# A four-layer graph-attention stack: the grid of v from weight lengths in three layers, and another order of sums, fillers and w rows

## What is computed

```
Wh = h @ W
e = u[:, None] + v[None, :]            # u = Wh @ a_src, v = Wh @ a_dst
e = where(e > 0, e, 0.2 * e)
attention = softmax(where(adj > 0, e, -9e15), axis=1)
out = elu(attention @ Wh)
```

## Time and profile before

| | |
|---|---|
| median of 3 runs | 678.42 us (673.24 to 678.65) |
| profiled execution, its own time | 678.56 us |
| span, first to last instruction | 676.5 us, 7526 instructions |
| mean granted TensorE clock | 0.934 |
| busy: TensorE, VectorE, ScalarE, GpSimd | 586.6, 366.5, 278.6, 29.1 us |

### The profile page before, as it was taken

How to read it: one execution, slowest core, us unless ns; L and a number is a source line. 1 busy time by engine, 2 the same in 40 slices (tenths; PEclk the granted TensorE clock), 3 DMA queues, 4 the chain that set the end, 5 groups by cost and what they waited for, 6 DMA issues and landing times.

```text
span 676.5 us, 7526 instructions
## 1 busy us (share of the span) xinstructions
PE 586.6 (87%) x3167; PEld 196.9 (29%) x3167; DVE 366.5 (54%) x515; ACT 278.6 (41%) x297; POOL 29.1 (4%) x27
## 2 busy tenths in 40 slices
PE   5434999998999998999979899988679898999997
PEld 3301222343222333122234122235223231333332
DVE  2876756537656537665644675624599968100001
ACT  1564545433545432544532554432577765200000
POOL 0400000200000100000000000012000000000000
PEclk9556999999999999899997899999699998899999
DMA  9990000000000000000000000000000000000000
GB/s 361 357 360 7 1 0 1 1 0 1 1 1 0 1 1 1 0 1 1 0 1 1 0 1 1 0 1 1 0 0 1 1 0 1 1 0 1 1 0 32
DMA packets 3041, 19.33 MB, mean 29 GB/s; under 512 B 320, under 2 KB 320, under 8 KB 960
## 3 DMA queue, kind: packets, MB, share of 16 engines
q1 hardware_dynamic: 2864, 17.83, 6.7%
q10 hardware_dynamic: 144, 1.03, 0.5%
HBM read 18.33 MB, written 0.52 MB: 28 GB/s over the span
## 4 chain that ended last, share of the span: by engine, by line
PE 64%; DVE 19%; ACT 7%; issue 5%; DMA 2%; POOL 1%; POOLq 0%; DVEq 0%; ACTq 0%
PE PROD L632 14%; PE X L842 8%; PE S L644 8%; PE X L624 8%; PE PROD L842 7%; DVE X L1064 5%; DVE aB L1273 5%; ACT big L362 3%; PE X L523 2%; PE M L610 2%; PE S L857 2%; DMA big<-in_adjT 2%; DVE big L1051 1%; DVE nadj L1172 1%; POOL rr L301 1%
## 5 line engine op out<-in xcount | busy, mean ns | idle before, releaser
L362 ACT ACTIVATE big<-X,v 128x1024 f32<-128x1024 f32 x128 | 137.3, 1111 | 154.9 <-PE X L624 154.4
L1064 DVE SCALAR_TENSOR_TENSOR X<-wB,v,aB 128x1024 f32<-128x1024 f32 x128 | 161.5, 1290 | 71.2 <-ACT big L362 69.8
L632 PE MATMUL PROD<-big,Wh 128*64 128x512 f32 x512 | 130.8, 631 | 3.6 <-ACT big L362 3.4
L624 PE MATMUL X<-nadj,bigI 128*128 128x512 bf16 x256 | 73.4, 391 | 23.9 <-DVE X L1064 23.7
L644 PE MATMUL S<-big,onesf 128*32 128x512 f32 x512 | 68.2, 605 | 5.3 <-ACT big L362 5.3
L632 PEld LDWEIGHTS PROD<-big,Wh 128*64 128x64 f32 x512 | 31.2, 139 | 84.9 <-ACT big L362 45.7
L624 PEld LDWEIGHTS X<-nadj,bigI 128*128 128x128 bf16 x256 | 16.3, 97 | 102.4 <-DVE X L1064 66.3
L842 PE MATMUL PROD<-nadj,Wh 128*64 128x512 f32 x128 | 31.0, 614 | 2.9 <-ACT nadj L458 2.9
L301 POOL TENSOR_TENSOR rr<-var,mhalf 128x8 f32<-128x8 f32 x8 | 16.9, 2114 | 377.2 <-DVE var L965 377.2
L610 PE MATMUL M<-big,level 128*32 128x512 fp8e4 x256 | 19.5, 440 | 15.4 <-ACT big L401 8.6
L842 PE MATMUL PROD<-big,Wh 128*64 128x512 f32 x128 | 31.3, 606 | 0.7 <-ACT big L458 0.6
(11 more groups left out here) (254 smaller groups left out, 583.4 us busy)
## 6 DMA issues: line engine op xcount, KB each, us to landing
big<-in_adjT SPq DMA_DIRECT2D x13, 1024.0 KB, 7.9
aB<-in_adjT SPq DMA_DIRECT2D x3, 1024.0 KB, 9.1
cst<-in_cst ACTq DMA_DIRECT2D x1, 1008.5 KB, 5.6
x<-in_xT SPq DMA_DIRECT2D x1, 512.0 KB, 6.2
out<-x SPq DMA_DIRECT2D x2, 256.0 KB, 2.0
```

The costliest lines, as they stand in the source:

```text
L362: act.activation(prob[:, t % U, :], X[t % 2][:], ACT.Exp, bias=v2[l % 2][:, k:k + 1]).then_inc(p_ready, 1)
L624: last = pe.matmul(X[t % 2][:, hh * BANK:(hh + 1) * BANK], bigI[:], nadj[:, k, half_cols(c, hh)], start=False, stop=True, skip_group_check ...
L632: last = pe.matmul(PROD[c][feat(hh), :], Wh[l % 2][:, k, :], prob[:, t % U, hh * BANK:(hh + 1) * BANK], start=k == 0, stop=k == NB - 1)
L1064: dve.scalar_tensor_tensor(X[t % 2][:], wB[:, cols(c)], v8[l % 2][:, k:k + 1], aB[:, cols(c)], ALU.max, ALU.add).then_inc(x_written, 1)
```

## The change

For the first three attention layers (`l < FIX`) the range of `v` is not found any more. `h` has a bounded length after normalisation, so `|v|` is at most that length times the length of the vector that makes `v` out of `h`. The kernel takes the squares of these weight vectors once, in the load (`weight_squares`), adds them up with one product on TensorE, takes the inverse root on GpSimd, and makes a bound, a step and its inverse for the three layers (`weight_norms`, `value_bounds`, which also give `nvs` and `nvb` for `shift_rows`). `value_levels` then makes `gridz` from `v` in one instruction. The grid is centred, so the constant `win` is shifted by half the span, and `LEAN` moves the result back. The last layer (`l == 3`) keeps the range, in a `value_range` of its own.

In the load `convert(5)` and `convert(6)`, which stood between the steps of the range, move behind layer 0's levels. On TensorE the sums of chunk 0's last pair move behind its products and behind the first two masks of chunk 1 (chunk 1's last pair keeps its order); the fillers ahead of the loop go from 12 to 19; between two loops the numbers of fillers change, and ahead of layer 3 `features` comes before `w_rows`. The hunks left out (...) declare tiles and semaphores.

```diff
@@ -24,6 +24,9 @@
 TOP = LOW + EXPS * 128
 SPAN = WIN * EXPS * 128 * (1 - 2.0 ** -12)
 SLOPE = 0.2
+FIX = 3
+REACH = 8.1
+LEAN = 5.5 * 128
 PARTS = 3
 KR = PARTS * PARTS * EMB
 KPAD = 96
...
@@ -312,6 +327,8 @@
 
             for c in range(NCH):
                 inverse_root(part_of(rr, c), part_of(var, c))
+            pool.wait_ge(normsq_ready, 1)
+            pool.tensor_tensor(norm[:], normsq[:], mhalf[:, 0:FIX], ALU.pow).then_inc(norm_ready, 1)
             for c in range(NCH):
                 below_one(c)
             for lf in (1, 2):
@@ -346,11 +363,11 @@
                     act.activation(wB[:, half_cols(c, hh)], row_bank(n, hh)[:], ACT.Copy).then_inc(wB_ready, 1)
 
             def shift_rows(l):
-                act.wait_ge(nv_param, l + 1)
+                act.wait_ge(nv_param, 1 + l // FIX)
                 for q in range(4):
                     act.wait_ge(nv_psum, 4 * l + q + 1)
                     act.activation(aB[:, q * BANK:(q + 1) * BANK], X[q // 2][:, (q % 2) * BANK:(q % 2 + 1) * BANK],
-                                   ACT.Identity, bias=nv[:, 1:2], scale=nv[:, 0:1]).then_inc(nv_ready, 1)
+                                   ACT.Identity, bias=nvb[:, l:l + 1], scale=nvs[:, l:l + 1]).then_inc(nv_ready, 1)
 
             def exponential(l, c, k):
                 t = NB * (NCH * l + c) + k
@@ -587,13 +604,12 @@
                     last = pe.matmul(EB[c][feat(hh), bb * P:(bb + 1) * P], col, ident, start=True, stop=True)
                 last.then_inc(rb_psum, 1)
 
-            def value_range(l):
-
-                pe.wait_ge(vext_ready, l + 1)
+            def value_range():
+
+                pe.wait_ge(vext_ready, 1)
                 pe.transpose(X[1][0:2, 0:P], vext[:], ident).then_inc(vrow_psum, 1)
-                if l:
-                    repeat(X[0], 3)
-                pe.wait_ge(diag_ready, l + 1)
+                repeat(X[0], 3)
+                pe.wait_ge(diag_ready, 1)
                 pe.matmul(X[1][:, 0:2], onef2[:], diag2[:], start=True, stop=True).then_inc(range_psum, 1)
 
             def top_levels(l):
@@ -708,6 +724,9 @@
                 centre(n)
             for n in range(NCH):
                 variances(n)
+            pe.wait_ge(wsq_ready, 1)
+            pe.matmul(X[1][:, 0:FIX], onesf[0:F, 0:1].broadcast_to([F, P]), wsq[:], start=True,
+                      stop=True).then_inc(norm_psum, 1)
             for n in range(NCH):
                 features(n)
             for n in range(NCH):
@@ -715,9 +734,7 @@
                 w_broadcast(n)
 
             for l in range(GAT):
-                if l == 0:
-                    value_range(0)
-                else:
+                if l == 3:
                     repeat(X[0], 9)
                 top_levels(l)
                 if l:
@@ -725,7 +742,7 @@
                 if l == 2:
                     root_broadcast(0)
                 if l:
-                    repeat(M, 12)
+                    repeat(M, 19)
                 pe.wait_ge(nv_ready, 4 * (l + 1))
                 mask(l, 0, 0)
                 mask(l, 0, 1)
@@ -734,7 +751,7 @@
                         k = 2 * p
                         if p == 0 and l == 2:
                             pe.wait_ge(h0_ready, c + 1)
-                        if p == NB // 2 - 1:
+                        if c and p == NB // 2 - 1:
                             pe.wait_ge(p_ready, NB * (NCH * l + c + 1))
                             sums(l, c, k + 1)
                         products(l, c, k)
@@ -742,10 +759,11 @@
                         if p < NB // 2 - 1:
                             mask(l, c, k + 2)
                             mask(l, c, k + 3)
-                            sums(l, c, k + 1)
                         elif c == 0:
                             mask(l, 1, 0)
                             mask(l, 1, 1)
+                        if c == 0 or p < NB // 2 - 1:
+                            sums(l, c, k + 1)
                         if c == 0:
                             if p == 0 and l:
                                 w_broadcast(2 * l + 1)
@@ -781,19 +799,21 @@
                 reciprocal_rows(l, 1)
                 if l < 2:
                     centre_old(2 * l + 3)
-                repeat(X[0], 2)
-                if l < 2:
+                    repeat(X[0], 3)
                     centre(2 * l + 3)
-                if l < 3:
                     w_rows(2 * l + 2)
-                if l < 2:
                     variances(2 * l + 3)
                     repeat(X[0], 2)
+                    features(2 * l + 3)
+                if l == 2:
+                    repeat(X[0], 12)
+                    features(2 * l + 3)
+                    w_rows(2 * l + 2)
                 if l < 3:
-                    features(2 * l + 3)
                     w_broadcast(2 * l + 2)
-                    repeat(X[0], 2)
-                    value_range(l + 1)
+                    repeat(X[0], 3 if l == 2 else 7)
+                if l == 2:
+                    value_range()
             first_turn(0)
             mlp(1)
             repeat(X[1], 3)
@@ -1013,30 +1033,65 @@
 
                 par = l % 2
                 v = uv[par][:, :, 1]
+                if l < FIX:
+                    signal(dve.scalar_tensor_tensor(gridz[:], v.unsqueeze(2).broadcast_to([P, NB, WIN]),
+                                                    istep[:, l:l + 1], win.unsqueeze(1).broadcast_to([P, NB, WIN]),
+                                                    ALU.mult, ALU.add), grid_ready, l + 1)
+                else:
+                    value_range()
+                dve.tensor_scalar(level[:].bitcast(i16), gridz[:], 0.0, float(TOP), ALU.max,
+                                  ALU.min).then_inc(level_ready, 1)
+                if l < FIX:
+                    shares(l)
+
+            def shares(l):
+
+                v = uv[l % 2][:, :, 1]
+                dve.tensor_scalar(v8[l % 2][:], v, 1 - SLOPE, None, ALU.mult)
+                dve.tensor_scalar(v2[l % 2][:], v, SLOPE, None, ALU.mult)
+
+            def value_range():
+
+                v = uv[1][:, :, 1]
                 dve.tensor_reduce(vext[:, 0:1], v, AX.X, ALU.max)
                 dve.tensor_reduce(vext[:, 1:2], v, AX.X, ALU.min, negate=True).then_inc(vext_ready, 1)
-                dve.tensor_scalar(v8[par][:], v, 1 - SLOPE, None, ALU.mult)
-                dve.tensor_scalar(v2[par][:], v, SLOPE, None, ALU.mult)
-                if l == 0:
-                    convert(5)
-                dve.wait_ge(vrow_psum, l + 1)
+                shares(3)
+                dve.wait_ge(vrow_psum, 1)
                 link(dve.tensor_reduce(rowx[:], X[1][0:2, 0:P], AX.X, ALU.max))
                 dve.tensor_scalar(diag2[:], ident[0:2, 0:2], rowx[:], None, ALU.mult).then_inc(diag_ready, 1)
-                if l == 0:
-                    convert(6)
-                dve.wait_ge(range_psum, l + 1)
+                dve.wait_ge(range_psum, 1)
                 link(dve.tensor_copy(rng[:, 0:2], X[1][:, 0:2]))
                 link(dve.tensor_scalar(rng[:, 2:3], rng[:, 0:1], rng[:, 1:2], 1e-30, ALU.add, ALU.max))
                 link(dve.tensor_scalar(rng[:, 2:3], rng[:, 2:3], 1.0 / SPAN, None, ALU.mult))
                 link(dve.reciprocal(rng[:, 3:4], rng[:, 2:3]))
                 link(dve.tensor_scalar(vz[:], v, rng[:, 1:2], rng[:, 3:4], ALU.add, ALU.mult))
-                link(dve.tensor_tensor(gridz[:], vz[:].unsqueeze(2).broadcast_to([P, NB, WIN]),
-                                       win.unsqueeze(1).broadcast_to([P, NB, WIN]), ALU.add))
-                dve.tensor_scalar(level[:].bitcast(i16), gridz[:], 0.0, float(TOP), ALU.max,
-                                  ALU.min).then_inc(level_ready, 1)
-                dve.tensor_scalar(nv[:, 0:1], rng[:, 2:3], -1.0, None, ALU.mult)
-                dve.tensor_scalar(nv[:, 1:2], rng[:, 2:3], float(LOW * WIN), rng[:, 1:2], ALU.mult,
+                signal(dve.scalar_tensor_tensor(gridz[:], vz[:].unsqueeze(2).broadcast_to([P, NB, WIN]), -SPAN / 2,
+                                                win.unsqueeze(1).broadcast_to([P, NB, WIN]), ALU.add, ALU.add),
+                       grid_ready, 4)
+                dve.tensor_scalar(nvs[:, 3:4], rng[:, 2:3], -1.0, None, ALU.mult)
+                dve.tensor_scalar(nvb[:, 3:4], rng[:, 2:3], float(LOW * WIN + LEAN), rng[:, 1:2], ALU.mult,
                                   ALU.add).then_inc(nv_param, 1)
+
+            def weight_squares():
+
+                dve.wait_ge(prep_ready, 3)
+                dst = wt4[0:F, 0:FIX, 0, F + 1:F + 2].rearrange("p l t -> p (l t)")
+                dve.tensor_tensor(wsq[:], dst, dst, ALU.mult).then_inc(wsq_ready, 1)
+
+            def weight_norms():
+                dve.wait_ge(norm_psum, 1)
+                dve.tensor_scalar(normsq[:], X[1][:, 0:FIX], 1e-30, None, ALU.max).then_inc(normsq_ready, 1)
+
+            def value_bounds():
+
+                dve.wait_ge(norm_ready, 1)
```

(19 more changed lines are left out.)

14 lines of the change are left out of this document (13 added, 1 removed).

## The result

The changed kernel takes 657.3 us (median of 4 runs, 656.7 to 659.68), the kernel before beside it 677.36 (673.24 to 678.65). The ratio is 0.9721 with a 95% interval of 0.967 to 0.9771. Three numbers go by the name of the gain: 20.1 us between the medians, 21.0 between the two profiled executions, and 21.4 in the forecast, which starts from the profiled 678.56.

What follows compares the result with a forecast made beforehand. TensorE's queue bounds the loops, short VectorE steps the stretches between, the last adjacency block the load. Load 1.2, grid 5.1, last transition 3.5, switch 6.6 and fillers 5.0 sum to 21.4: 678.56 to 657.2 us, range 652 to 664.

Steps and rivals of the forecast that it cites:

- The grid: Layers 1 and 2: computing the grid straight from v starts the level products 2.55 us earlier each, 5.1 us.
- The last transition: Into layer 3: features ahead of w_rows and fillers at full clock bring the level products 3.5 us earlier.
- The switch: Chunk 0 to chunk 1, once a layer: the new order removes two TensorE waits, 1.65 us each, 6.6 us.
- The rival that gives half back: At the chunk switch: a mask or exponential comes late, 4 x 0.88 lost, 660.7 us; chance 0.11.
- Fillers: Ahead of the first mask, layers 1 to 3: nineteen for twelve keep the clock full, gaining 5.0 us.
- The load: Loading the adjacency: last block lands at 51.7 for 52.95, 1.2 us gained.
- the late block 10 costs: In the load: block 10's transfer, issued at 32.8 instead of 30.48, might push later blocks, at worst to about 53.7.
- The clock falls anyway: Rival: the clock falls despite the fillers, losing the 5.0: 662.2 us, or 663.9 with the last transition's drop; chance 0.16.
- The load ends later: Rival: block 10's late issue is not made up, load ends at 53.7, 2.0 lost, 659.2 us; chance 0.08.

Runs made afterwards that it cites:

- e4: The kernel before with all of the change but the grid from weight lengths (range in all four layers, old load): 662.75 us, ratio 0.9777.
- e3: The changed kernel with TensorE's old order between layers 2 and 3 (two fillers, w rows, then features): 658.16 us, ratio 0.9721.
- e12: The kernel before with ten fillers at the very start of TensorE's program and nothing else: 677.45 us, ratio 0.9971.
- e1: The changed kernel with the old order of chunk 0's last pair (sums, products, then chunk 1's masks): 662.63 us, ratio 0.9785.
- e2: The changed kernel with 12 fillers in place of 19 ahead of the loops of layers 1 to 3: 660.43 us, ratio 0.9759.
- e6: The changed kernel with convert(5) and convert(6) ahead of value_bounds in the load: 656.14 us, ratio 0.9655.
- e7: The changed kernel with value_range ahead of the w broadcast on TensorE before layer 3: 657.65 us, ratio 0.9665.
- e9: The changed kernel with ten start fillers, value_range ahead of the w broadcast before layer 3, and five fillers for nine behind it: 651.82 us, ratio 0.9622.
- e10: As e9, with 18 fillers ahead of layer 0's loop: 650.52 us, ratio 0.959.
- e5: The changed kernel with ten fillers at the very start of TensorE's program: 654.29 us, ratio 0.9622.

## Why the prediction was right, step by step

657.2 was forecast and 657.3 measured. The mechanisms of the grid, the last transition and the switch held. That the sum came out to 0.1 us is luck: the load was missed by 2.9 us, the tail gave 2.0 back, and the forecast started from an execution of 678.56 where the median beside the changed kernel is 677.36.

- **The grid, 5.1 us**: right in mechanism and size; 5.3 in the traces, 5.4 by e4. The one wrong detail: the extra filler ahead of `centre` costs 0.05 us and not 0.22 (from the last exponential to the last `uv`); the reason was not tested. The assumption that the new grid instruction costs 0.69 held nearly (0.75).
- **The last transition, 3.5 us**: 3.4, with the late `vext` transpose where the queue order put it. But e3 lost only 2.2 of them: the rest hung on the length of one low stretch, 10.2 us in the traces of before and of e12, 6.8 in e3.
- **The switch, 6.6 us**: 7.2. The rows held to a tenth; I had rounded 1.7 down to 1.65, and it is 1.8 in each layer. e1 shows the waits as its cause. The rival that gives half back fell.
- **Fillers, 5.0 us**: 4.9 in the pair of traces, so the term met. As a statement on the edit it was too sure: e2 loses 2.0 us in its trace and nothing in layer 1, and e12, whose instructions there are those of before, shows no loss in layer 1 either (14.21) and 2.8 us in the other two. The forecast took one profile's falls for what happens each time: of the three traces with twelve fillers it had the costliest. This is the size that a range should have carried.
- **The load, 1.2 us gained**: the step that failed. The trace shows 1.7 lost up to the 7th exponential of layer 0, a miss of 2.9. It failed twice. First, "the late block 10 costs": e6 asks for it 2.4 us sooner and wins nothing. Second, it took the first variances, and all that stands behind them in VectorE's queue, as they stood in the trace of before. They run the same instructions in both kernels and took 1.05 us in one profile and 1.87 in the other, and block 10 went out at 35.59 where 32.8 was forecast. In e1, which has the changed load and variances of 1.05 us, it went out at 33.00 and the last block landed at 50.55, within the forecast's 50.5 to 51.9. What the change itself wins in the load stays open: the same new load writes its first `X` between 60.81 and 64.56 without a warm start, which is more than the 1.2 us in question.
- **The tail, not in the sum**: 2.0 us shorter in the trace after, of which e12 puts 1.6 down to nothing in the change. It hid most of the load's miss. The other 0.4 lie among the chain of keys ahead of the first scores, a stretch that spreads over 2 us between kernels with the same instructions there. In e3, e7, e9 and e12, which are the long ones, it holds one more stretch of 3.4 us at 1.2 GHz; the smaller differences are open.
- **Rivals**: none came. "The clock falls anyway" was refused: behind waits of 0.49, 1.19 and 0.49 us the three layers take 14.21 us. "The load ends later" gave the right sign and the wrong cause.

What stays open is why the first variances were fast in two of the ten profiles without the ten fillers and slow in eight. They stand behind the same instructions; the ten fillers made them fast in all four kernels that had them (in e10 nearly, 1.24 us).

## What to carry to other kernels

Where two engines hand work to each other at the end of a chunk, put what the next chunk's first step waits for ahead of what only frees buffers: that was worth 1.8 us a switch, read to a tenth from one stretch of the timeline. Compare traces stretch by stretch between the same events before the totals: a total that fits can hold a miss of 3 us and 2 us of luck against it. And price an edit that is meant for the clock from several profiles, for one shows only one way that it can fall.

## What the runs showed of the hardware

- How fast TensorE's products ran in the first 20 us of an execution reached a transfer-bound end 38 us later, over VectorE's queue: 3 us on the last convert between two traces of the same load (53.49 in the changed kernel, 50.57 in e1).
- The granted share is no witness until the profile has its first record of the clock; ahead of it the share reads 1.00. In the changed kernel's trace it does so from 15.2 to 18.0, while the variances took 1.87 us. That these ran at the lower level is read from durations: a group of eight small products ahead of them took 1.86 us in e10, where the profile does record a share of 0.50, and 1.05 in e5, where it records 1.00. The durations are the surer witness there. Windows of before and of the changed kernel:

```profile
15.20:18.00 2.80, 2.77 (x23) 2.77 (x24) 2.34 (x5) 0.47 (x1) 1.02 (x1) 0.95 1.01 421
```

```profile
15.20:18.00 2.80, 2.64 (x13) 2.64 (x13) 1.55 (x3) 0.60 (x2) 0.34 (x1) 1.00 1.01 421
```

- The first record stands at 14.3 us in the trace of before and at 15.5 in e1, ahead of their fast variances, between 22.9 and 24.2 in seven of the eight profiles with slow ones, and at 5.1 to 6.6 with the ten fillers. In e3 there is none before 72.5: its share reads 1.00 over the whole load, though the first products of layer 0 take 3.68 us, as in the changed kernel, where the share beside them is 0.50. So the mean shares of two kernels (0.956 and 0.934; 0.982 in e3's slower profile) don't compare as they stand. e3, the window and the products:

```profile
55.00:70.00 15.00, 8.56 (x30) 1.96 (x28) 9.01 (x10) 5.01 (x6) 0.00 (x0) 1.00 0.00 0
```

```profile
68.09 3.68 PE L648 MATMUL PROD<-big,Wh 128*64 128x512 f32 x8
```

- In the tail one stretch of 3.4 us at 1.2 GHz cost 1.6 to 1.7 us: 138.29, 139.97 and 141.59 us with none, one and two of them.
- The same idle stretch of 2.00 us with a further 0.52 behind it was followed by a fall to 1.2 GHz in layer 1 of the trace of before and not in e2 nor in e12; in layer 3 a fall followed it in all three. Such a stretch puts the clock at risk, it doesn't decide it.
- VectorE steps beside GpSimd's `xq` steps took 0.57, 0.55 and 0.26 us in the changed kernel's trace for 0.17 or 0.18, three again as before, and a convert of 1.22 took 1.63 as they began. By the rule of the Trainium skill (SBUF — State Buffer, Who interferes with whom) a step with two SBUF inputs could have waited out a whole `xq` step of 1.8 us. This trace doesn't bear it out: the two-input steps at 25.36 and 25.77, beside the second `xq` step, took their usual 0.17, the slowed ones have one input each, and 0.41 is the most that one of them lost. In the trace of before one of the three slowed steps had two inputs, and took 0.53.
